# The last state's transposes behind the next batch's late neighbours: an order change in a graph-attention and GRU kernel

## The chip, the cores and the metric

The kernel runs on one core of a Trainium2 chip. The metric is the device time of one launch in microseconds (us). The engines have a queue each and run beside one another: TensorE (PE, with its weight loads as PEld), VectorE (DVE), ScalarE (ACT), GpSimd (POOL), and SyncE (SP), which here issues all DMAs. An instruction that waits for a semaphore holds up everything behind it on its engine.

## The reference

Eight batches of a graph with 1024 nodes and 128 features each. `x` is a layer-norm and ReLU away from a graph attention; its result is added to `x`; the sum goes through a layer-norm and ReLU into three gated graph layers with a GRU cell; and the last state is added again.

```python
h = jnp.maximum(_layernorm(x), 0.0)
Wh = h @ W
e = leaky(e_i[:, :, None] + e_j[:, None, :])       # e_i = Wh.a1, e_j = Wh.a2, slope 0.2
attention = softmax(where(adj > 0, e, -9e15), axis=2)
x = x + elu(attention @ Wh)
h = jnp.maximum(_layernorm(x), 0.0)                # h0 below
A = (adj != 0)
for i in range(3):
    aggr = einsum('bst,bsd->btd', A, h @ weight[i])
    r, z = sigmoid(i_r + h_r), sigmoid(i_z + h_z)  # gi = aggr @ w_ih.T + b_ih, gh = h @ w_hh.T + b_hh
    n = tanh(i_n + r * h_n)
    h = (1 - z) * n + z * h
x = x + h
```

## The kernel before, in words

Work is written by hand, one program for each engine, each with a `first()` for what comes ahead and a `body(b, ...)` that is run for the eight batches. The order of the calls in `body` is the order on the engine; semaphores with counts join the engines. Body `b` does the three GRU layers of batch `b` and, between them, the attention of the next batch `a = b + 1` and the first steps of batch `b + 2`. `attend` is true while there is a batch `a` (all but the last body), `prepare` while there is a batch `b + 2` (bodies 0 to 5).

A batch is 8 tiles of 128 nodes, or two halves of 512 (`c` = 0 and 1). In the GRU the state is kept with features on partitions (`hkT`, and `h0T` for the first), split into a high and a low part for exact matmuls. One layer goes: the neighbours' sum `ps_g` (16 matmuls of 128x512 for each half of source tiles: `neighbours(b, par, l, k, c)` takes source half `k` to target half `c`, 8 matmuls), its split (`g_hi` on ACT, `g_lo_half` on DVE), nine matmuls of the old state and nine of the sum for each half (`gates_h`, `gates_g`), the gates (`r_gate`, `z_gate`, `n_gate` on ACT, `n_input` on DVE), `z_times_h` on POOL, `new_h` on DVE, which writes `hkT`, and the transpose back (`h_back` on PE). After the last layer the transposed halves go into PSUM banks `ps_hn` and `ps_r`, and `out_half` on DVE adds `x1` and leaves the output for the store. The next batch's first nine state matmuls write `ps_hn` again and wait until both `out_half` are done.

The end of a body, called the tail here, is where the GRU of batch `b` ends and that of `a` begins. For the second half of `a`'s first state it runs: `att_half`, `x1_sum` (DVE, the residual), `norm2` (DVE, statistics), `rstd2_half` (POOL, with a power), `h0_half` (ACT), then `split_h0` (DVE) for the neighbour matmuls and `h0T_half` (PE transposes, ACT copy) with `split_h` (POOL) for the state matmuls. In `neighbours(a, a_par, 0, k, c)` the source half `k = 0` ("early") needs the first half of `h0`, and `k = 1` ("late") the second.

Around the tail stand attention steps of batch `b + 2`: `leaky_tile` (ACT) writes a tile of scores, `away_tile` (DVE) makes the mask from the adjacency, `scores` (DVE) adds them and takes the row maximum, `exp_tile` (ACT) follows, and `probT_tile` transposes on PE. `norm1` (DVE) and `rstd1` (POOL) are the first layer-norm of batch `b + 2`. Lines of the profile that matter: L969 neighbours, L912 transposes, L978 to L980 gate matmuls; L646 away, L652 edges, L662 scores, L698 and L704 statistics of `norm2`, L714 and L716 `split_h0`, L721 `g_lo`, L727 and L730 `n_input`, L737 and L740 `new_h`, L751 `out_half`; L366 `h0_half`; L275 to L280 `rstd_of`, L300 and L302 `z_times_h`, L312 and L315 `split_h`.

Of the kernel before, what the change touches and what calls it, by code (L numbers as in the profile page):

```python
# [21 lines left out]
def gat_gru_kernel(nc, x, adj, gat_w, gat_a, layer_w, w_ih, w_hh, b_ih, b_hh, out):  # L22
# [6 lines left out]
    QS = 2 * L  # L29
# [9 lines left out]
    with ExitStack() as ctx:  # L39
# [224 lines left out]
        @block.gpsimd  # L264
        def _(pool):
            pool.memset(minus_half[:], -0.5)
            pool.memset(ident[:], 0.0).then_inc(const_done, 1)
            pool.wait_ge(const_done, 1)
            pool.affine_select(out=ident[:], in_=ident[:], compare_op=ALU.not_equal, fill=1.0, base=0,
                               pattern=[[-1, P]], channel_multiplier=1).then_inc(const_done, 1)  # L270
            pool.wait_ge(const_done, 2)

            def rstd_of(dst, minus, mean_var, k, n, added, powered, done):

                pool.tensor_scalar(dst, mean_var[:, :, 1], LN_EPS, 1.0, ALU.add, ALU.mult).then_inc(added, 1)  # L275
                pool.tensor_scalar(minus, mean_var[:, :, 0], -1.0, 0.0, ALU.mult, ALU.add)
                pool.wait_ge(added, n)
                pool.tensor_tensor(dst, dst, minus_half[:, 0:k], ALU.pow).then_inc(powered, 1)  # L278
                pool.wait_ge(powered, n)
                pool.tensor_tensor(minus, minus, dst, ALU.mult).then_inc(done, 1)  # L280

            def rstd1(b):
                pool.wait_ge(mv_done, b + 1)
                if b > 0:
                    pool.wait_ge(h_done, b * 2)
                rstd_of(rstd[:], shift[:], mv, T, b + 1, vare_done, pow_done, rstd_done)

            def rstd2_half(b, c):
                n = b * 2 + c + 1
                pool.wait_ge(mv2_done, n)  # L290
                if n > 1:
                    pool.wait_ge(h0_done, n - 1)
                rstd_of(rstd2[:], shift2[:], mv2, TH, n, vare2_done, pow2_done, rstd2_done)

            def z_times_h(b, l, c):

                n = b * QS + 2 * l + c + 1
                h = h0T if l == 0 else hkT
                pool.wait_ge(tz_done, n)
                pool.tensor_scalar(tz[c][:], tz[c][:], 0.5, 0.5, ALU.mult, ALU.add).then_inc(z_done, 1)  # L300
                pool.wait_ge(z_done, n)
                pool.tensor_tensor(zh[c][:], tz[c][:], h[:, cols(c)], ALU.mult).then_inc(zh_done, 1)  # L302

            def split_h(b, l, c):

                n = b * QS + 2 * l + c + 1
                h = h0T if l == 0 else hkT
                if l == 0:
                    pool.wait_ge(h0T_done, b * 2 + c + 1)
                else:  # L310
                    pool.wait_ge(hk_done, n - 2)
                pool.tensor_scalar(hT_hi[:, cols(c)], h[:, cols(c)], 1.0, 0.0, ALU.mult, ALU.add  # L312
                                   ).then_inc(hT_hi_done, 1)
                pool.wait_ge(hT_hi_done, n)
                pool.tensor_tensor(hT_lo[:, cols(c)], h[:, cols(c)], hT_hi[:, cols(c)], ALU.subtract  # L315
                                   ).then_inc(hT_lo_done, 1)

            def first():
                rstd1(0)
                rstd1(1)  # L320
                rstd2_half(0, 0)
                split_h(0, 0, 0)
                rstd2_half(0, 1)
                split_h(0, 0, 1)

            def body(b, par, attend, prepare):
                if prepare:
                    rstd1(b + 2)
                for l in range(L - 1):
                    z_times_h(b, l, 0)  # L330
                    z_times_h(b, l, 1)
                    split_h(b, l + 1, 0)
                    split_h(b, l + 1, 1)
                if attend:
                    rstd2_half(b + 1, 0)
                z_times_h(b, L - 1, 0)
                z_times_h(b, L - 1, 1)
                if attend:
                    rstd2_half(b + 1, 1)
                    split_h(b + 1, 0, 0)  # L340
                    split_h(b + 1, 0, 1)

            run(pool, first, body)


        @block.scalar
        def _(act):
# [10 lines left out]
            def h0_half(b, par, c):  # L358

                n = b * 2 + c + 1  # L360
                act.wait_ge(rstd2_done, n)
                if n > 1:
                    act.wait_ge(h0T_ps, n - 1)
                    act.wait_ge(h0_lo_done, n - 1)
                for t in range(TH):
                    last = act.activation(h0[:, t, :], x1[par][:, c * TH + t, :], ACT.Relu, bias=shift2[:, t:t + 1],  # L366
                                          scale=rstd2[:, t:t + 1])
                last.then_inc(h0_done, 1)
# [55 lines left out]
            def r_gate(b, l, c):  # L424

                act.wait_ge(r_ps, b * QS + 2 * l + c + 1)
                act.activation(tr[c][:], ps_r[:], ACT.Tanh, bias=b_rz[:, 0:1], scale=0.5).then_inc(tr_done, 1)  # L427

            def z_gate(b, l, c):
                act.wait_ge(z_ps, b * QS + 2 * l + c + 1)  # L430
                act.activation(tz[c][:], ps_z[:], ACT.Tanh, bias=b_rz[:, 1:2], scale=0.5).then_inc(tz_done, 1)  # L431

            def n_gate(b, l, c):
                if l == 0:
                    act.wait_ge(stored[c], b * 16 + 1)
                act.wait_ge(pre_done, b * QS + 2 * l + c + 1)
                act.activation(nn[c][:], pre[c][:], ACT.Tanh, bias=bih_in[:, 2:3]).then_inc(n_done, 1)  # L437
# [36 lines left out]
            def body(b, par, attend, prepare):  # L474
# [88 lines left out]
                r_gate(b, 2, 0)  # L563
                z_gate(b, 2, 0)
                hnb_half(b, 2, 1)
                n_gate(b, 2, 0)
                r_gate(b, 2, 1)
                z_gate(b, 2, 1)
                n_gate(b, 2, 1)
                if prepare:  # L570
                    leaky_tile(b + 2, par, 0)
                if attend:
                    h0_half(a, a_par, 1)
                    h0T_half(a, a_par, 1)
                if prepare:
                    leaky_tile(b + 2, par, 1)
# [5 lines left out]
        def _(dve):  # L582
# [66 lines left out]
            def edge_tile(b, par, t):  # L649


                dve.tensor_scalar(edges[par][:, t, :], adj_in[t % TA][:], 0.0, None, ALU.not_equal  # L652
                                  ).then_inc(edges_done, 1)
# [76 lines left out]
                dve.tensor_tensor(pre[c][:], pre[c][:], ps_in[:], ALU.add).then_inc(pre_done, 1)  # L730

            def new_h(b, l, c):

                n = b * QS + 2 * l + c + 1
                dve.wait_ge(z_done, n)
                dve.wait_ge(n_done, n)
                dve.scalar_tensor_tensor(nn[c][:], tz[c][:], 1.0, nn[c][:], ALU.subtract, ALU.mult).then_inc(zn_done, 1)  # L737
                dve.wait_ge(zn_done, n)
                dve.wait_ge(zh_done, n)
                dve.tensor_tensor(hkT[:, cols(c)], zh[c][:], nn[c][:], ALU.subtract).then_inc(hk_done, 1)  # L740
# [38 lines left out]
            def body(b, par, attend, prepare):  # L779
                a, a_par = b + 1, 1 - par  # L780

                if attend:
                    scores(a, 0)
                    away_tile(a, a_par, 1)
                    scores(a, 1)
                if prepare:
                    norm1(b + 2, par)
# [56 lines left out]
                g_lo_half(b, 2, 1)  # L844
                if attend:
                    split_h0(a, 0)
                    att_half(a, a_par, 1)
                    x1_sum(a, a_par, 1)
                n_input(b, 2, 0)
                if attend:  # L850
                    norm2(a, a_par, 1)
                    new_h(b, 2, 0)
                    n_input(b, 2, 1)
                else:
                    new_h(b, 2, 0)
                    n_input(b, 2, 1)
                new_h(b, 2, 1)
                if attend:
                    split_h0(a, 1)
                out_half(b, par, 0)  # L860
                if prepare:
                    away_tile(b + 2, par, 0)
                out_half(b, par, 1)

            run(dve, first, body)

# [2 lines left out]
        def _(pe):  # L869
# [191 lines left out]
            def body(b, par, attend, prepare):  # L1061
# [10 lines left out]
                    neighbours(b, par, l, 1, 1)  # L1072


                late_neighbours(0)
                if attend:
                    probT_tile(a, a_par, 0)
                gates_h(b, 0, 0)
# [51 lines left out]
                gates_g(b, 2, 0)  # L1130
                gates_h(b, 2, 1)
                gates_g(b, 2, 1)
                h_back(b, 2, 0)
                if attend:
                    neighbours(a, a_par, 0, 0, 0)
                h_back(b, 2, 1)
                if attend:
                    neighbours(a, a_par, 0, 0, 1)
                    h0T_half(a, a_par, 1)

            run(pe, first, body)


# [23 lines left out]
```

## Time and profile before

| | |
|---|---|
| median of 3 runs | 695.64 us (695.63 to 695.66) |
| the profiled execution's own time | 695.68 us |
| its span, first to last instruction | 693.9 us |
| PE busy | 623.9 us (90%) |
| DVE busy | 521.4 us (75%) |
| ACT busy | 453.2 us (65%) |
| POOL busy | 282.2 us (41%) |

Times inside the trace are from the start of the span. Matmuls are pipelined: one of 128x512 is shown with about 0.40 us, and the next starts some 0.24 us after it. In a row of the order of time the second column is the duration, and the bracket at the end is how long the engine stood idle before the row, and what ended that.

### The profile page before, as it was taken

The page shows a single profiled execution, that of the slowest core. Times are in us where ns is not written, and L with a number is a line of the kernel's source. Part 1 is how long each engine was busy: PE and PEld are TensorE (multiplying, and loading weights), DVE is VectorE, ACT ScalarE, POOL GpSimd, SP SyncE. Part 2 cuts the span into 40 slices and gives each one's busy share as a digit, 9 for nine tenths or more (in the row PEclk, how much of TensorE's full clock was granted, in tenths as well). Part 3 has the DMA queues.
Part 4 walks back from the last instruction along what each step waited for, and adds up shares of the span by engine and source line. Part 5 has one row for each costly group of instructions (what it writes and reads, how often), then busy time and mean ns, then how long its engine had stood idle before and what let it go on. Part 6 is the DMA issues. An engine that isn't in the chain of part 4 may idle for free.

```text
span 693.9 us, 8823 instructions
## 1 busy us (share of the span) xinstructions
PE 623.9 (90%) x2845; PEld 457.0 (66%) x2845; DVE 521.4 (75%) x1218; ACT 453.2 (65%) x777; POOL 282.2 (41%) x295
## 2 busy tenths in 40 slices
PE   2687899989999899988999889997999899998996
PEld 2465677667686676666776666866766677766774
DVE  5766998489876898669985798768986689656544
ACT  2784786558874678557864588756785577554443
POOL 1203544166242561544442662425615434425442
PEclk9999999999999999999999999999999999999999
DMA  6521130122302132022401223021320131001001
GB/s 222 180 92 61 44 139 31 47 77 92 112 10 92 31 122 92 31 62 67 146 32 45 78 92 95 28 91 31 121 92 27 34 94 60 0 1 30 1 1 30
DMA packets 28670, 47.40 MB, mean 68 GB/s; under 512 B 1672, under 2 KB 19408, under 8 KB 28624
## 3 DMA queue, kind: packets, MB, share of 16 engines
q1 hardware_dynamic: 28624, 46.84, 20.3%
q8 instruction: 23, 0.38, 0.2%
q14 instruction: 23, 0.19, 0.1%
HBM read 42.60 MB, written 4.23 MB: 67 GB/s over the span
## 4 chain that ended last, share of the span: by engine, by line
PE 52%; DVE 20%; ACT 11%; POOL 10%; issue 5%; DMA 1%; DVEq 0%; POOLq 0%; ACTq 0%
PE ps_x L931 14%; PE ps_g L969 8%; PE ps_x L912 6%; DVE score L662 4%; POOL rstd L278 3%; DVE away L646 3%; POOL zh L302 3%; DVE hkT L740 2%; ACT score L390 2%; PE ps_r L978 2%; PE ps_r L980 2%; PE ps_r L979 2%; DVE nn L737 2%; PE ps_z L978 2%; PE ps_z L979 2%
## 5 line engine op out<-in xcount | busy, mean ns | idle before, releaser
L969 PE MATMUL ps_g<-edges,h_hi 128*128 128x512 f32 x384 | 157.8, 411 | 11.7 <-DVE h_lo L746 6.6
L969 PE MATMUL ps_g<-edges,h_lo 128*128 128x512 f32 x384 | 151.9, 396 | 0.0
L300 POOL TENSOR_SCALAR tz<-tz 128x512 f32<-128x512 f32 x48 | 37.0, 771 | 253.8 <-ACT tz L431 253.8
L390 ACT ACTIVATE score<-score,nmax 128x1024 f32<-128x1024 f32 x64 | 73.8, 1153 | 43.8 <-DVE nmax L662 42.8
L931 PE MATMUL ps_x<-probT,h_nat 128*128 128x512 f32 x224 | 98.9, 594 | 0.0
L662 DVE CUSTOM_DVE_ANT_0 score<-score,away 128x1024 f32<-128x1024 f32 x64 | 89.0, 1390 | 8.0 <-ACT score L384 7.0
L969 PEld LDWEIGHTS ps_g<-edges,h_hi 128*128 128x128 f32 x384 | 72.8, 189 | 31.2 <-DVE h_lo L746 10.3
L912 PE MATMUL ps_x<-ident,score 128*128 128x128 f32 x512 | 71.6, 282 | 17.4 <-ACT score L390 16.2
L397 ACT ACTIVATE probT<-ps_x 128x512 f32<-128x512 f32 x128 | 71.0, 597 | 17.3 <-PE ps_x L912 17.2
L969 PEld LDWEIGHTS ps_g<-edges,h_lo 128*128 128x128 f32 x384 | 72.9, 190 | 13.6
L912 PEld LDWEIGHTS ps_x<-ident,score 128*128 128x128 f32 x512 | 59.4, 145 | 34.1 <-ACT score L390 25.4
L384 ACT ACTIVATE score<-ej,ei 128x1024 f32<-128x1024 f32 x64 | 73.0, 1143 | 6.0 <-DMA ej<-ej_kept_at 5.0
L931 PEld LDWEIGHTS ps_x<-probT,h_nat 128*128 128x128 f32 x224 | 41.9, 190 | 50.3 <-issue 46.9
L646 DVE TENSOR_SCALAR away<-adj_in 128x1024 bf16<-128x1024 int32 x64 | 61.6, 963 | 0.0
L315 POOL TENSOR_TENSOR hT_lo<-hkT,hT_hi 128x512 fp32r<-128x512 f32 x32 | 56.9, 1777 | 2.7
L275 POOL TENSOR_SCALAR rstd<-mv 128x4 f32<-128x4 f32 (+1 forms) x24 | 7.5, 312 | 122.5 <-DVE mv L704 75.1
L737 DVE SCALAR_TENSOR_TENSOR nn<-tz,nn 128x512 f32<-128x512 f32 x48 | 37.2, 775 | 24.0 <-ACT nn L437 24.0
L437 ACT ACTIVATE nn<-tr,vec 128x512 f32<-128x512 f32 x48 | 34.8, 725 | 28.0 <-DVE tr L730 26.7
L652 DVE TENSOR_SCALAR edges<-adj_in 128x1024 fp32r<-128x1024 int32 x64 | 50.6, 799 | 0.0
L366 ACT ACTIVATE h<-x,shift,rstd 128x128 f32<-128x128 f32 x64 | 26.4, 482 | 32.5 <-POOL shift L280 32.5
L721 DVE TENSOR_TENSOR g_lo<-ps_g,g_hi 128x512 fp32r<-128x512 f32 x48 | 31.6, 680 | 19.7 <-ACT g_hi L417 19.7
L727 DVE SCALAR_TENSOR_TENSOR tr<-tr,hnb 128x512 f32<-128x512 f32 x48 | 35.9, 748 | 11.7 <-ACT tr L427 11.6
(133 smaller groups left out, 1314.0 us busy)
## 6 DMA issues: line engine op xcount, KB each, us to landing
adj_in<-in_adj SPq DMA_DIRECT2D x64, 512.0 KB, 3.3
x_nat<-in_x SPq DMA_DIRECT2D x8, 512.0 KB, 4.7
ej<-ej_kept_at SPq DMA_DIRECT2D x8, 512.0 KB, 3.6
out<-nn SPq DMA_DIRECT2D x16, 256.0 KB, 2.3
probT<-in_L_gnn_weight SPq DMA_DIRECT2D x1, 192.0 KB
probT<-in_L_gnn_w_ih SPq DMA_DIRECT2D x1, 192.0 KB
probT<-in_L_gnn_w_hh SPq DMA_DIRECT2D x1, 192.0 KB
ej_kept_at<-ej_row SPq DMA_DIRECT2D x8, 4.0 KB
```

Source lines behind the costliest of these rows:

```text
L300: pool.tensor_scalar(tz[c][:], tz[c][:], 0.5, 0.5, ALU.mult, ALU.add).then_inc(z_done, 1)
L315: pool.tensor_tensor(hT_lo[:, cols(c)], h[:, cols(c)], hT_hi[:, cols(c)], ALU.subtract).then_inc(hT_lo_done, 1)
L384: act.activation(score[t % U][:], ej[:], ACT.Prelu, bias=ei[par][:, t:t + 1], alpha=SLOPE).then_inc(leaky_done, 1)
L390: act.activation(score[t % U][:], score[t % U][:], ACT.Exp, bias=nmax[:, t:t + 1], scale=-1.0, accum_out=rowsum[:, t:t + 1]).then_inc(exp_ ...
L397: act.activation(probT[:, k * TH:(k + 1) * TH, tile_cols(t % TH)], bank_of("probT", 2 * t + k, par)[:].rearrange("p (j i) -> p j i", j=TH) ...
L646: dve.tensor_scalar(away[t % 2][:], adj_in[t % TA][:], 0.0, -K, ALU.is_le, ALU.mult).then_inc(away_done, 1)
L652: dve.tensor_scalar(edges[par][:, t, :], adj_in[t % TA][:], 0.0, None, ALU.not_equal).then_inc(edges_done, 1)
L662: dve.tensor_tensor_reduce(u[:], u[:], away[t % 2][:], -1.0, FLT_BIG, ALU.add, ALU.min, nmax[:, t:t + 1]).then_inc(max_done, 1)
L737: dve.scalar_tensor_tensor(nn[c][:], tz[c][:], 1.0, nn[c][:], ALU.subtract, ALU.mult).then_inc(zn_done, 1)
L912: last = pe.transpose(dst[:, tile_cols(t)], src, ident[:])
L931: last = pe.matmul(bank_of("agg", c, par)[:], h_nat[par][:, j, :], probT[:, j, :], start=(j == 0), stop=(j == T - 1))
L969: last = pe.matmul(ps_g[c][:], part[:, s, :], edges[par][:, s, cols(c)], start=(s == 0 and part is h_hi), stop=(s == T - 1 and part is h_lo))
```

## The change

Nothing is computed that was not computed before; calls move. On PE the two `h_back` of the last layer leave the tail of body `b` and stand in body `b + 1`, each behind one half of the late neighbours. On POOL the second `rstd2_half` goes ahead of both `z_times_h`. On ACT `h0_half(a, a_par, 1)` goes ahead of the second `n_gate`, and the first `n_gate` behind the second `r_gate`. On DVE the second `norm2` follows its `x1_sum` at once, `new_h` of the last layer's first half is cut in two with `split_h0(a, 1)` between, `scores(b + 2, 0)` comes ahead of the last `new_h`, `away_tile(b + 2, 0)` goes ahead of the second `att_half`, and both `out_half` go to the next body, the second behind `away_tile(a, a_par, 1)`. In layer 0 one `edge_tile` goes behind `new_h`.

```diff
 # POOL
                 if attend:
                     rstd2_half(b + 1, 0)
+                if attend:
+                    rstd2_half(b + 1, 1)
                 z_times_h(b, L - 1, 0)
                 z_times_h(b, L - 1, 1)
                 if attend:
-                    rstd2_half(b + 1, 1)
                     split_h(b + 1, 0, 0)
 # ACT (condition on attend left out of n_gate)
-                n_gate(b, 2, 0)
                 r_gate(b, 2, 1)
+                    n_gate(b, 2, 0)
                 z_gate(b, 2, 1)
+                if attend:
+                    h0_half(a, a_par, 1)
                 n_gate(b, 2, 1)
                 if prepare:
                     leaky_tile(b + 2, par, 0)
                 if attend:
-                    h0_half(a, a_par, 1)
                     h0T_half(a, a_par, 1)
 # DVE, start of the body
-                if attend:
+                if b == 0:
                     scores(a, 0)
+                else:
+                    out_half(b - 1, a_par, 0)
+                if attend:
                     away_tile(a, a_par, 1)
+                if b > 0:
+                    out_half(b - 1, a_par, 1)
+                if attend:
                     scores(a, 1)
...
                     edge_tile(a, a_par, 1)
+                new_h(b, 0, 0)
+                if attend:
                     edge_tile(a, a_par, 2)
-                new_h(b, 0, 0)
 # DVE, tail
+                if prepare:
+                    away_tile(b + 2, par, 0)
+                if attend:
                     att_half(a, a_par, 1)
-                    x1_sum(a, a_par, 1)
-                n_input(b, 2, 0)
-                if attend:
-                    norm2(a, a_par, 1)
+                    x1_half(a, a_par, 1)
+                    n_input(b, 2, 0)
+                    n_input(b, 2, 1)
+                    n_part(b, 2, 0)
+                    split_h0(a, 1)
+                    h_sum(b, 2, 0)
...
+                if prepare:
+                    scores(b + 2, 0)
                 new_h(b, 2, 1)
-                if attend:
-                    split_h0(a, 1)
-                out_half(b, par, 0)
-                if prepare:
-                    away_tile(b + 2, par, 0)
-                out_half(b, par, 1)
+                if not attend:
+                    out_half(b, par, 0)
+                    out_half(b, par, 1)
 # PE, start of the body
-                late_neighbours(0)
+                neighbours(b, par, 0, 1, 0)
+                if b > 0:
+                    h_back(b - 1, 2, 0)
+                neighbours(b, par, 0, 1, 1)
+                if b > 0:
+                    h_back(b - 1, 2, 1)
 # PE, tail
-                h_back(b, 2, 0)
                 if attend:
                     neighbours(a, a_par, 0, 0, 0)
-                h_back(b, 2, 1)
-                if attend:
                     neighbours(a, a_par, 0, 0, 1)
                     h0T_half(a, a_par, 1)
```

PE in the tail of body 0, from the last gate matmul to the first score transposes of the next body, before (`ps_hn` and `ps_r` take the old batch's transposes, `ps_x1` those of `h0`; of each run of eight neighbour matmuls the first stands):

```order
L980 MATMUL ps_in<-g_hi1,cT_lo 128x512
L912 MATMUL ps_hn<-ident,hkT 128x128 x4
L969 MATMUL ps_g0<-edges1,h_hi 128x512
...
L912 MATMUL ps_r<-ident,hkT 128x128 x4
L969 MATMUL ps_g1<-edges1,h_hi 128x512
...
L912 MATMUL ps_x1<-ident,h0 128x128 x4
...
L912 MATMUL ps_x0<-ident,score0 128x128 x4
```

The same place of the changed program, where the lines are numbered 23 higher:

```order
L1003 MATMUL ps_in<-g_hi1,cT_lo 128x512
L992 MATMUL ps_g0<-edges1,h_hi 128x512
...
L935 MATMUL ps_x1<-ident,h0 128x128 x4
L992 MATMUL ps_g0<-edges1,h_hi 128x512
...
L935 MATMUL ps_hn<-ident,hkT 128x128 x4
L992 MATMUL ps_g1<-edges1,h_hi 128x512
...
L935 MATMUL ps_r<-ident,hkT 128x128 x4
L935 MATMUL ps_x0<-ident,score0 128x128 x4
```

All 16 early neighbour matmuls now come directly behind the gates, and the two groups of `hkT` transposes behind eight late ones each.

DVE at the same place before, from the first half's `new_h` (`nn0`, `hkT<-zh0`) to the next batch's first `scores`:

```order
L737 SCALAR_TENSOR_TENSOR nn0<-tz0,nn0 128x512
L740 TENSOR_TENSOR hkT<-zh0,nn0 128x512
L727 SCALAR_TENSOR_TENSOR tr1<-tr1,hnb1 128x512
L730 TENSOR_TENSOR tr1<-tr1,ps_in 128x512
L737 SCALAR_TENSOR_TENSOR nn1<-tz1,nn1 128x512
L740 TENSOR_TENSOR hkT<-zh1,nn1 128x512
L714 TENSOR_SCALAR h_hi<-h0 128x512
L716 TENSOR_TENSOR h_lo<-h0,h_hi 128x512
L751 TENSOR_TENSOR nn0<-ps_hn,x1_0 128x512
L646 TENSOR_SCALAR away0<-adj_in0 128x1024
L751 TENSOR_TENSOR nn1<-ps_r,x1_0 128x512
L662 ISA score0,nmax<-score0,away0 128x1024
```

And in the changed program, from the second half's `n_input` to the second output sum:

```order
L735 TENSOR_TENSOR tr1<-tr1,ps_in 128x512
L746 SCALAR_TENSOR_TENSOR nn0<-tz0,nn0 128x512
L719 TENSOR_SCALAR h_hi<-h0 128x512
L721 TENSOR_TENSOR h_lo<-h0,h_hi 128x512
L753 TENSOR_TENSOR hkT<-zh0,nn0 128x512
L667 ISA score0,nmax<-score0,away0 128x1024
L667 ISA nmax 128x1
L746 SCALAR_TENSOR_TENSOR nn1<-tz1,nn1 128x512
L753 TENSOR_TENSOR hkT<-zh1,nn1 128x512
L764 TENSOR_TENSOR nn0<-ps_hn,x1_0 128x512
L651 TENSOR_SCALAR away1<-adj_in1 128x1024
L764 TENSOR_TENSOR nn1<-ps_r,x1_0 128x512
```

The split of `h0` comes ahead of both `hkT` halves, the first score ahead of the second half's `new_h`, and the mask between the output sums is that of tile 1 instead of tile 0.

## Rows read from the trace of the kernel before

**Rows 1.** Stretches: length, then PE, PEld, DVE, ACT, POOL busy us (count), clock, DMA.

```profile
231.20:240.20 9.00, 7.49 (x38) 5.79 (x38) 8.86 (x26) 5.59 (x9) 2.50 (x3) 1.00 0.22 60
240.20:264.10 23.90, 22.38 (x111) 17.35 (x110) 23.44 (x34) 20.19 (x36) 13.61 (x12) 1.00 0.34 113
264.10:300.00 35.90, 35.86 (x158) 24.10 (x157) 23.81 (x74) 22.08 (x41) 11.69 (x12) 1.00 0.12 45
```

**Rows 2.** PE by time, tail of the second body: start, us, engine, line, [idle before].

```profile
225.14 0.66 PE L912 MATMUL ps_hn<-ident,hkT 128*128 128x128 f32 x4 [0.38 <-DVE hkT L740]
225.55 0.48 PE L969 MATMUL ps_g<-edges,h_hi 128*128 128x512 f32 x1
...
229.16 0.66 PE L912 MATMUL ps_r<-ident,hkT 128*128 128x128 f32 x4 [1.50 <-DVE hkT L740]
...
232.55 0.50 PE L969 MATMUL ps_g<-edges,h_hi 128*128 128x512 f32 x1 [0.46 <-DVE h_lo L716]
...
237.54 1.09 PE L912 MATMUL ps_x<-ident,score 128*128 128x128 f32 x8 [1.05 <-ACT score L390]
...
240.95 0.50 PE L978 MATMUL ps_r<-g_hi,cT_hi 128*128 128x512 f32 x1 [0.22 <-DVE g_lo L721]
```

**Rows 3.** DVE by time, the same tail.

```profile
218.02 1.13 DVE L674 TENSOR_SCALAR att<-ps_x,rinv 128x128 f32<-128x128 f32 x4 [2.85 <-PE ps_x L952]
...
221.18 0.68 DVE L727 SCALAR_TENSOR_TENSOR tr<-tr,hnb 128x512 f32<-128x512 f32 x1
...
222.50 0.86 DVE L698 BATCH_NORM_STATS2 stats<-x 128x6 f32<-128x128 f32 x4
223.40 0.38 DVE L704 BATCH_NORM_AGGREGATE mv<-stats 128x2 f32<-128x6 f32 x4
...
227.68 0.69 DVE L737 SCALAR_TENSOR_TENSOR nn<-tz,nn 128x512 f32<-128x512 f32 x1 [0.86 <-ACT nn L437]
...
231.24 0.53 DVE L714 TENSOR_SCALAR h_hi<-h 128x512 fp32r<-128x512 f32 x1 [2.14 <-ACT h L366]
...
232.41 0.68 DVE L751 TENSOR_TENSOR nn<-ps_hn,x 128x512 f32<-128x512 f32 x1
233.01 0.96 DVE L646 TENSOR_SCALAR away<-adj_in 128x1024 bf16<-128x1024 int32 x1
...
234.49 1.72 DVE L662 CUSTOM_DVE_ANT_0 score<-score,away 128x1024 f32<-128x1024 f32 x1
...
236.85 1.23 DVE L662 CUSTOM_DVE_ANT_0 score<-score,away 128x1024 f32<-128x1024 f32 x1
238.00 0.08 DVE L662 DVE_READ_ACCUMULATOR2_ANT nmax<- 128x1 f32 x1
...
240.24 1.25 DVE L721 TENSOR_TENSOR g_lo<-ps_g,g_hi 128x512 fp32r<-128x512 f32 x2
```

**Rows 4.** ACT by time, the same tail.

```profile
224.10 0.69 ACT L431 ACTIVATE tz<-ps_z,b_rz 128x512 f32<-128x512 f32 x1
...
227.48 1.13 ACT L384 ACTIVATE score<-ej,ei 128x1024 f32<-128x1024 f32 x1
229.55 1.65 ACT L366 ACTIVATE h<-x,shift,rstd 128x128 f32<-128x128 f32 x4 [0.94 <-POOL shift L280]
```

**Rows 5.** POOL by time, the same tail.

```profile
222.43 1.30 POOL L302 TENSOR_TENSOR zh<-tz,hkT 128x512 f32<-128x512 f32 x1
...
227.34 0.19 POOL L275 TENSOR_SCALAR rstd<-mv 128x4 f32<-128x4 f32 x1
```

**Rows 6.** DVE by time, layer 0 of the third body: a mask.

```profile
252.84 1.77 DVE L646 TENSOR_SCALAR away<-adj_in 128x1024 bf16<-128x1024 int32 x1
```

**Rows 7.** POOL by time, the same moment.

```profile
252.46 1.59 POOL L315 TENSOR_TENSOR hT_lo<-hkT,hT_hi 128x512 fp32r<-128x512 f32 x1
```

**Rows 8.** PE by time, the last tail.

```profile
629.09 0.39 PE L980 MATMUL ps_in<-g_hi,cT_lo 128*128 128x512 f32 x1
...
641.07 0.39 PE L978 MATMUL ps_hn<-hT_hi,whhT_hi 128*128 128x512 f32 x1
```

More of the change, by code:

```diff
@@ L565, in body @@
                 hnb_half(b, 2, 1)
-                n_gate(b, 2, 0)
+                if not attend:
+                    n_gate(b, 2, 0)
                 r_gate(b, 2, 1)
+                if attend:
+                    n_gate(b, 2, 0)
                 z_gate(b, 2, 1)
+                if attend:
+                    h0_half(a, a_par, 1)
                 n_gate(b, 2, 1)
@@ L732, in new_h, with n_part @@
             def new_h(b, l, c):
+                n_part(b, l, c)
+                h_sum(b, l, c)
+            def n_part(b, l, c):
                 n = b * QS + 2 * l + c + 1
@@ L737, in new_h, with h_sum @@
                 dve.scalar_tensor_tensor(nn[c][:], tz[c][:], 1.0, nn[c][:], ALU.subtract, ALU.mult).then_inc(zn_done, 1)
+            def h_sum(b, l, c):
+                n = b * QS + 2 * l + c + 1
                 dve.wait_ge(zn_done, n)
@@ L780, in body @@
                 a, a_par = b + 1, 1 - par
+                if b == 0:
+                    scores(a, 0)
+                else:
+                    out_half(b - 1, a_par, 0)
                 if attend:
-                    scores(a, 0)
                     away_tile(a, a_par, 1)
+                if b > 0:
+                    out_half(b - 1, a_par, 1)
+                if attend:
                     scores(a, 1)
@@ L846, in body @@
                     split_h0(a, 0)
+                if prepare:
+                    away_tile(b + 2, par, 0)
+                if attend:
                     att_half(a, a_par, 1)
-                    x1_sum(a, a_par, 1)
-                n_input(b, 2, 0)
-                if attend:
-                    norm2(a, a_par, 1)
+                    x1_half(a, a_par, 1)
[4 more added lines that the diff above has]
+                    h_sum(b, 2, 0)
+                else:
+                    n_input(b, 2, 0)
                     new_h(b, 2, 0)
                     n_input(b, 2, 1)
-                else:
-                    new_h(b, 2, 0)
-                    n_input(b, 2, 1)
+                if prepare:
+                    scores(b + 2, 0)
                 new_h(b, 2, 1)
-                if attend:
-                    split_h0(a, 1)
-                out_half(b, par, 0)
-                if prepare:
-                    away_tile(b + 2, par, 0)
-                out_half(b, par, 1)
+                if not attend:
+                    out_half(b, par, 0)
+                    out_half(b, par, 1)
             run(dve, first, body)
@@ L1132, in body @@
                 gates_g(b, 2, 1)
-                h_back(b, 2, 0)
                 if attend:
                     neighbours(a, a_par, 0, 0, 0)
-                h_back(b, 2, 1)
-                if attend:
                     neighbours(a, a_par, 0, 0, 1)
                     h0T_half(a, a_par, 1)
+                else:
+                    h_back(b, 2, 0)
+                    h_back(b, 2, 1)
             run(pe, first, body)
```

## The prediction

> **What bounds the kernel now.** I read the busy time by stretches first. From 264 to 300 us of the third body PE has no idle time (35.86 of 35.90 us). From 240 to 264 it stands 1.5 us, and there DVE is full (23.44 of 23.90); from 231 to 240 DVE is full too (8.86 of 9.00), while PE idles 1.5 us [rows 1]. So a body is bound by PE for its later part, and by DVE for some 33 us from the end of the tail on. The granted clock is at its upper level in each stretch.
>
> Next I read PE in order of time through the tail of the second body, which stands for all seven tails (bodies 0 to 6). PE waits five times: 0.38 and 1.50 us for `hkT`, 0.46 for the split `h0`, 1.05 for the first exponential, 0.22 for `g_lo` [rows 2]; together 3.6 us. The last wait is short, but it ends last: whatever PE gains earlier, the first gate matmul on `g` (240.95) cannot start before DVE's first `g_lo` (240.24) is done.
>
> So DVE's own row of work decides. It waits 2.14 us for the second half of `h0` until 231.24, and from there it works without a pause to `g_lo` [rows 3]: 9.0 us for the split, two output sums, a mask, two scores, a mask and the statistics of `norm1`. The half of `h0` is late because ACT writes it at 229.55 to 231.20 [rows 4], behind POOL's `rstd2`, which starts only at 227.34 [rows 5], though its statistics are ready at 223.78 (223.40 and 0.38, [rows 3]): POOL does both `z_times_h` first.
>
> **The change, part by part.** Times are those of this tail, so a difference is a gain per tail.
>
> *The second half of h0.* `norm2` no longer stands behind `n_input`, which took from 221.18 to 222.50 [rows 3], so the statistics end 1.3 us earlier, at 222.5. POOL takes them at once; its four instructions and the hand-over to ACT take 2.2 us (227.34 to 229.55, [rows 4, 5]): 224.7. ACT is not free then. Its second `z_gate`, 224.10 to 224.79 [rows 4], now has a tanh of the same size ahead of it and ends near 225.5; with 1.65 us, `h0` is done near 227.2 instead of 231.2, 4 us earlier. Queued behind it on ACT are the second `n_gate` and the first leaky tile (1.13 us, [rows 4]), which end about 229.0. On POOL both `z_times_h` move behind `rstd2`: about 0.7 and 1.3 us each [rows 5], so near 227 and 229.
>
> *PE.* Sixteen matmuls from 232.55 end at 236.49 (237.54 less 1.05), so one starts 0.236 us after another ((3.94 - 0.40) / 15), and four transposes take 0.41 (225.14 to 225.55) [rows 2]. The gates can be followed at 224.60 (225.14 less 0.38, less 0.16 by which the last matmul's modelled 0.40 overlaps the next). Now come 16 early matmuls (3.78) to 228.4, the `h0` transposes to 228.8, eight late ones to 230.7, the first `hkT` transposes to 231.1, eight late ones to 233.0, and the second `hkT` transposes, which end 0.66 later, 233.6. Nothing in this row has to wait: `h0` is there at 227.2, its split (1.17 us on DVE, 231.24 to 232.41) at 228.4, 0.4 before the late ones. The waits of 0.38, 1.50 and 0.46 go; the new places of the `hkT` transposes cost no instruction.
>
> *DVE.* Behind `h0` at 227.2 now stand: the split (1.17), the first half's difference (0.69 like its neighbour at 227.68), the first score (1.15 as at 236.85 to 238.00, or the 1.72 of the row at 234.49), the second half's `new_h` (two of 0.69), the first output sum (0.60), a mask (0.96) [rows 3]. That ends between 233.1 and 233.7, just when PE's last transposes do (233.6). From there the order leaves no choice: output sum 0.68, score 1.15, `norm1` 2.24 (238.00 to 240.24), and `g_lo` starts at 237.8 instead of 240.24: 2.4 to 2.5 us earlier. PE would come to it at about 236.5 (probabilities 0.85, nine state matmuls 2.1), so I expect a new wait of about 2 us there in place of the 0.22. The state matmuls also wait for the second output sum, by some 0.2 us.
>
> *The mask of tile 0* (0.96) goes ahead of `att_half`, where DVE stands idle 2.85 us for PE [rows 3]: nothing, and nothing if the cover shrank by half. Without cover it costs 0.96 per tail.
>
> *The edge tile behind new_h of layer 0* is in DVE's full stretch: the same instructions in another order, so zero for `g`. Bounds: PE could get `hkT` one edge tile (0.7) earlier, or the next `n_input` be 0.7 later; I take zero, since DVE has no gap to give.
>
> *DMAs.* None is added. The two output stores are issued in the next body, ahead of the next adjacency load as before, and that load waits for edges that DVE makes only after `g_lo`. I take nothing.
>
> *Collisions of DVE and POOL.* A mask at 252.84 takes 1.77 us instead of 0.96 or less, beside a POOL subtraction at 252.46 to 254.05 [rows 6, 7], so a full collision costs DVE 0.8 to 1.1 us; the score at 234.49 is 0.5 over the one at 236.85. In the new order POOL works from 224.7 to about 233 without a gap (two `z_times_h`, two `split_h`, each about 2 us), and DVE's split, difference, score, `new_h` and mask lie beside it. Before, the same stretch had idle time of DVE beside `split_h`. Some of it is in the sum already (1.72, 0.96); the bounds of the rest are -0.9 (the collisions of the layer behind lapse, by re-phasing) and +1.9 (two more full ones). I take 0.3, near to the partial ones that this tail shows.
>
> By the Trainium skill (SBUF — State Buffer, "Who interferes with whom") whichever of a VectorE instruction with two SBUF inputs, or in a two-port mode, and a GpSimd instruction comes first holds their shared ports, and the other blocks until it is done. The 1.77 us agree with that. By the rule alone all four 1.3 us POOL products and subtractions could each hold up one DVE instruction; with two more of 1.3 than now nothing of a tail's 2.5 would be left but the last tail's 2.0, about 693.7 by this estimate.
>
> *Sum.* 2.5 - 0.3 = 2.2 us in each of the six tails with a batch `b + 2`: 13.2. The last tail has no score, mask or `norm1`. There PE is behind the gates at 629.32 (629.09 + 0.39 - 0.16); the same row of matmuls brings its second `hkT` transposes to 637.7, their end to 638.4, the output sum to 639.1, and the state matmuls start there instead of at 641.07 [rows 8]: 2.0. The first body's start and the last batch keep their order. Together 15.2 us of the profiled execution's 695.68 (span 693.9, and 1.8 around it, which stay): 680.5. The median of the runs is 0.04 below that execution, which changes nothing.
>
> **The rivals.**
>
> *More gain.* If no collision is left in the new tail and the shifted phase also loosens those in layer 0, a tail gives up to 3.3 us: 6 x 3.3 + 2.0 = 21.8, 673.9 us. For it: 1 us and more stands in single stretched rows. Against: PE's transposes at 233.6 and the 4.1 us of DVE work behind them are a floor for `g_lo`, so 2.5 is all that the tail itself can give.
>
> *Collisions take it.* One to two more full ones in DVE's row (0.9 each) leave about 1.2 a tail: 6 x 1.2 + 2.0 = 9.2, 686.5 us. For it: POOL now runs right through that row. Against: the first score has 0.4 us of slack before PE's transposes are done, and the second score and `norm1` come when POOL is through.
>
> *It doesn't matter.* The body is paced elsewhere (the adjacency loads, the row of `ej`), and what the tail gives is waited for later: 695. Against: no DMA ends a wait of PE or DVE in these stretches.
>
> *Slower.* In the new order 10.3 us of DVE work stand between `h0` and `g_lo` (1.17 + 0.69 + 1.4 + 1.4 + 0.6 + 0.96 + 0.68 + 1.15 + 2.24), before 9.0. It decides against the change from the point where `h0` is less than 1.3 us earlier than now, after 229.9. If `h0` stayed at 231.2, because ACT held it up behind the gates or POOL's power came late again, each of the six tails would lose 1.3 us: 695.7 + 7.8 = 703.5 with nothing gained in the last. Against: three engines would each have to add a microsecond.
>
> **How the numbers follow.** My forecast, 1.8 to 2.6 us a tail (its own range 678.1 to 682.9): 62%. More gain: 12%. Collisions take most: 18%. No difference: 3%. Slower: 5%. A measurement of this kernel can tell 0.2% (1.4 us) from no change. Faster is thus 92%, the same 3%, slower 5%. The range takes most of the second and third case: 675 to 687.
>
> **What would show it.** PE: the waits of 1.50 and 0.46 gone, `hkT` transposes without a wait or with a few tenths; a wait of 1.5 to 2.3 us for `g_lo` in the first gate matmul, six times. DVE: the wait for `h0` under 1 us. ACT: `h0_half` ending near 227.2 on this tail's clock, and hardly a wait for `rstd2`. POOL: no wait for DVE's statistics longer than 1 us. The prediction is wrong if `h0` is later than 230, if the second `hkT` half comes after PE wants it (233.0) by more than 0.7, or if the gain is seen in the tail and waited for again after 240.

## The result, and the profile of the changed kernel

The changed kernel takes 697.82 us (median of 7 runs), the kernel before 695.66: ratio 1.0029, interval 1.002 to 1.0039. It is slower by 0.2 to 0.4%, where 680.5 (675 to 687) had been forecast. The profiled span went from 693.9 to 696.0 us. The granted clock does not explain it: a run of the changed kernel at 0.994 took 698.58, one at 0.986 took 697.82, and in the 20 us behind the last gate matmul it is 1.00 in all seven tails of both kernels.

Page of the changed kernel, busy time by engine and two groups of DVE (line, instruction | busy, mean ns):

```profile
PE 624.0 (90%) x2845; PEld 457.6 (66%) x2845; DVE 547.5 (79%) x1218; ACT 452.3 (65%) x777; POOL 293.2 (42%) x295
...
L746 DVE SCALAR_TENSOR_TENSOR nn<-tz,nn 128x512 f32<-128x512 f32 x48 | 48.5, 1011 | 19.0 <-ACT nn L438 19.0
...
L753 DVE TENSOR_TENSOR hkT<-zh,nn 128x512 f32<-128x512 f32 x48 | 46.7, 973 | 1.4
```

DVE runs the same 1218 instructions but is busy 547.5 us instead of 521.4. `nn<-tz,nn` means 1011 ns instead of 775, `hkT<-zh,nn` 973 instead of 789. Instructions have become longer, and the tail shows which. Line numbers are higher than before by 23 on PE, 5 to 13 on DVE and 1 on ACT; times below are again of the second body's tail, where the last gate matmul starts at 224.75 (before 224.37, 0.38 earlier).

PE by time, the rows of the tail with a wait (they answer to [rows 2]):

```profile
230.12 0.50 PE L992 MATMUL ps_g<-edges,h_hi 128*128 128x512 f32 x1 [0.86 <-DVE h_lo L721]
...
236.08 0.66 PE L935 MATMUL ps_r<-ident,hkT 128*128 128x128 f32 x4 [1.55 <-DVE hkT L753]
...
237.88 0.50 PE L1001 MATMUL ps_hn<-hT_hi,whhT_hi 128*128 128x512 f32 x1 [0.27 <-DVE nn L764]
...
241.83 0.50 PE L1001 MATMUL ps_r<-g_hi,cT_hi 128*128 128x512 f32 x1 [1.59 <-DVE g_lo L726]
```

All four are for DVE, 4.3 us together where there were 3.6. The `hkT` transposes wait 1.55 us in a place where they were to come without a wait, and the first gate matmul on `g` starts 17.08 us behind the last gate matmul, before 16.58 (240.95 less 224.37).

DVE by time, from the last `n_input` sum to `g_lo` (answers to [rows 3]):

```profile
225.25 0.69 DVE L735 TENSOR_TENSOR tr<-tr,ps_in 128x512 f32<-128x512 f32 x1 [0.21 <-PE ps_in L1003]
225.85 1.76 DVE L746 SCALAR_TENSOR_TENSOR nn<-tz,nn 128x512 f32<-128x512 f32 x1
227.54 0.85 DVE L719 TENSOR_SCALAR h_hi<-h 128x512 fp32r<-128x512 f32 x1
228.42 1.64 DVE L721 TENSOR_TENSOR h_lo<-h,h_hi 128x512 fp32r<-128x512 f32 x1
229.99 1.09 DVE L753 TENSOR_TENSOR hkT<-zh,nn 128x512 f32<-128x512 f32 x1
231.00 2.32 DVE L667 CUSTOM_DVE_ANT_0 score<-score,away 128x1024 f32<-128x1024 f32 x1
...
233.25 1.09 DVE L746 SCALAR_TENSOR_TENSOR nn<-tz,nn 128x512 f32<-128x512 f32 x1
234.38 1.65 DVE L753 TENSOR_TENSOR hkT<-zh,nn 128x512 f32<-128x512 f32 x1
235.94 0.68 DVE L764 TENSOR_TENSOR nn<-ps_hn,x 128x512 f32<-128x512 f32 x1
...
237.14 0.68 DVE L764 TENSOR_TENSOR nn<-ps_r,x 128x512 f32<-128x512 f32 x1
...
241.11 1.26 DVE L726 TENSOR_TENSOR g_lo<-ps_g,g_hi 128x512 fp32r<-128x512 f32 x2
```

And POOL beside it (answers to [rows 5]):

```profile
222.91 0.54 POOL L275 TENSOR_SCALAR rstd<-mv 128x4 f32<-128x4 f32 x1 [10.46 <-DVE mv L709]
...
225.06 0.62 POOL L300 TENSOR_SCALAR tz<-tz 128x512 f32<-128x512 f32 x1
225.77 1.30 POOL L302 TENSOR_TENSOR zh<-tz,hkT 128x512 f32<-128x512 f32 x1
227.03 1.07 POOL L300 TENSOR_SCALAR tz<-tz 128x512 f32<-128x512 f32 x1
228.19 1.33 POOL L302 TENSOR_TENSOR zh<-tz,hkT 128x512 f32<-128x512 f32 x1
229.49 1.06 POOL L312 TENSOR_SCALAR hT_hi<-h0T 128x512 fp32r<-128x512 f32 x1
230.63 1.62 POOL L315 TENSOR_TENSOR hT_lo<-h0T,hT_hi 128x512 fp32r<-128x512 f32 x1
232.21 1.59 POOL L312 TENSOR_SCALAR hT_hi<-h0T 128x512 fp32r<-128x512 f32 x1
233.89 1.59 POOL L315 TENSOR_TENSOR hT_lo<-h0T,hT_hi 128x512 fp32r<-128x512 f32 x1
```

Read the two in pairs. From 225.77 on POOL works without a gap until 235.48, and its seven large instructions lie beside seven of DVE's, one to one. Beside the four with two inputs (1.30 to 1.62) DVE's `nn`, `h_lo`, score and `hkT` take 1.76, 1.64, 2.32, 1.65, where rows without POOL give 0.69 and, for the score, 1.22: 1.07 + 0.95 + 1.10 + 0.96 = 4.1 us. Beside the three with one input (1.07, 1.06, 1.59) DVE's `h_hi`, `hkT`, `nn` take 0.85, 1.09, 1.09 instead of 0.43 and 0.69: 1.2 us. Together 5.3 us in one tail. As POOL ends, DVE's instructions are short again.

The ends of the fourteen instructions (start plus duration) alternate strictly: POOL 227.07, DVE 227.61, POOL 228.10, DVE 228.39, and so on to POOL 235.48 and DVE 236.03. Each end comes a little less behind the other engine's than the instruction takes alone (DVE 0.53 to 0.55 us, `h_hi` 0.29, the score 1.07; POOL 0.48 or 0.49 with one input, 1.13 to 1.17 with two). So the 10.3 us from 225.77 to 236.03 are the sum of what the two do one after the other, about 6.2 of POOL and 4.1 of DVE.

The whole program agrees. The score transposes ahead of layer 1's state matmuls of one body and the next were 81.16 us apart before and are 81.83 apart now, in five bodies: +3.4. The start gives 0.44 back, the sixth period 0.52, the end 0.34: +2.1, the 696.0 less 693.9 of the spans. Of the 0.67 a body, 0.50 are there at the first gate matmul on `g`.

### The profile page after: what moved, and what is told of

It reads as the page before. It is cut to its first block, busy times and chain, and to the rows that moved or that the text cites. A ratio compares the mean times of both kernels' runs of the same rounds, so it can differ in the third digit from the quotient of the medians.

```text
span 696.0 us, 8823 instructions
## 1 busy us (share of the span) xinstructions
PE 624.0 (90%) x2845; PEld 457.6 (66%) x2845; DVE 547.5 (79%) x1218; ACT 452.3 (65%) x777; POOL 293.2 (42%) x295
## 3 DMA queue, kind: packets, MB, share of 16 engines
HBM read 42.60 MB, written 4.23 MB: 67 GB/s over the span
## 4 chain that ended last, share of the span: by engine, by line
PE 46%; DVE 28%; POOL 11%; ACT 9%; issue 5%; DMA 1%; DVEq 0%; ACTq 0%; POOLq 0%
PE ps_x L954 14%; PE ps_g L992 9%; DVE score L667 5%; PE ps_x L935 5%; DVE hkT L753 5%; POOL zh L302 4%; DVE nn L746 3%; POOL rstd L278 3%; ACT score L391 2%; POOL tz L300 2%; PE ps_x L975 2%; DVE away L651 2%; DVE stats L626 2%; PE ps_r L1001 2%; PE ps_z L1001 2%
## 5 line engine op out<-in xcount | busy, mean ns | idle before, releaser
L300 POOL TENSOR_SCALAR tz<-tz 128x512 f32<-128x512 f32 x48 | 38.8, 807 | 179.6 <-ACT tz L432 179.6
L667 DVE CUSTOM_DVE_ANT_0 score<-score,away 128x1024 f32<-128x1024 f32 x64 | 93.2, 1456 | 7.1 <-ACT score L385 6.3
L275 POOL TENSOR_SCALAR rstd<-mv 128x4 f32<-128x4 f32 (+1 forms) x24 | 9.9, 414 | 196.6 <-DVE mv L709 147.7
L746 DVE SCALAR_TENSOR_TENSOR nn<-tz,nn 128x512 f32<-128x512 f32 x48 | 48.5, 1011 | 19.0 <-ACT nn L438 19.0
L651 DVE TENSOR_SCALAR away<-adj_in 128x1024 bf16<-128x1024 int32 x64 | 59.2, 925 | 0.0
L753 DVE TENSOR_TENSOR hkT<-zh,nn 128x512 f32<-128x512 f32 x48 | 46.7, 973 | 1.4
L428 ACT ACTIVATE tr<-ps_r,b_rz 128x512 f32<-128x512 f32 x48 | 33.0, 688 | 21.9 <-PE ps_r L1003 21.9
L732 DVE SCALAR_TENSOR_TENSOR tr<-tr,hnb 128x512 f32<-128x512 f32 x48 | 32.9, 686 | 13.8 <-ACT tr L428 13.8
```

What stands on the lines that cost most here:

```text
L651: dve.tensor_scalar(away[t % 2][:], adj_in[t % TA][:], 0.0, -K, ALU.is_le, ALU.mult).then_inc(away_done, 1)
L667: dve.tensor_tensor_reduce(u[:], u[:], away[t % 2][:], -1.0, FLT_BIG, ALU.add, ALU.min, nmax[:, t:t + 1]).then_inc(max_done, 1)
```

## Experiments

Theory C (collisions): the tail would give what was forecast, but DVE and POOL hold each other up. Rivals: the edge tile moved in layer 0 costs it (E), or the new order itself is too long for DVE and no collision matters (the prediction's own "slower"). All ratios are to the kernel before, run alongside (medians 695.82 to 696.12 us).

**1 to 3: POOL's work made short.** The diff is against the changed kernel; the three differ in which of the four calls get the width 16. They leave out most of `z*h`, of the split, or of both, and serve to measure, not to be used.

```diff
-                z_times_h(b, L - 1, 0)
-                z_times_h(b, L - 1, 1)
+                z_times_h(b, L - 1, 0, 16 if attend else HALF)   # 1, 2
+                z_times_h(b, L - 1, 1, 16 if attend else HALF)   # 1, 2
                 if attend:
-                    split_h(b + 1, 0, 0)
-                    split_h(b + 1, 0, 1)
+                    split_h(b + 1, 0, 0, 16)   # 1, 3
+                    split_h(b + 1, 0, 1, 16)   # 1, 3
```

Both short (1): 

> The changed kernel, with the POOL instructions of the tail (the last layer's two z_times_h of bodies 0 to 6, and the two split_h of the next batch's first state) cut from 512 to 16 columns; this leaves out most of z*h and of the state's split there. Collision theory: DVE's ten instructions from the first half's product to the last new_h lose their 5.3 us of stretching a tail, g_lo starts when PE's last transposes allow it (2.5 us earlier than in the kernel before), 677 to 681 us. Rival, the order itself: the DVE row behind h0 is longer by 1.3 us and PE waits for it whatever POOL does, 694 to 698 us.

Products alone (2): 

> As x1_pool_short, but only the two z_times_h of the tail are cut to 16 columns (leaves out most of z*h there); the splits are whole. Collision theory: the two collisions of the products (the first half's product in DVE 1.76 us instead of 0.68, the split of h0 2.4 instead of 1.2) go, those of the two splits (score and last new_h) stay in part: 682 to 688 us. If the products alone were the loss: 677 to 679. If they were nothing: 696 to 698.

Splits alone (3): 

> As x1_pool_short, but only the two split_h are cut to 16 columns (leaves out most of the split of the state there). Collision theory: DVE is where it was up to the split of h0, then its first score loses 1.1 us and its last new_h 1.3, so g_lo starts about 2.4 us earlier: 680 to 685 us. If the splits alone were the loss: 677 to 679. If they were nothing: 696 to 698.

Measured: 677.42 us, ratio 0.9738 (0.9724 to 0.9753); 683.09, 0.9814 (0.9798 to 0.983); 684.85, 0.9842 (0.9828 to 0.9857). DVE by time with both short:

```profile
223.01 0.68 DVE L748 SCALAR_TENSOR_TENSOR nn<-tz,nn 128x512 f32<-128x512 f32 x1
224.25 0.43 DVE L721 TENSOR_SCALAR h_hi<-h 128x512 fp32r<-128x512 f32 x1 [0.55 <-ACT h L369]
224.71 0.69 DVE L723 TENSOR_TENSOR h_lo<-h,h_hi 128x512 fp32r<-128x512 f32 x1
225.32 0.68 DVE L755 TENSOR_TENSOR hkT<-zh,nn 128x512 f32<-128x512 f32 x1
226.01 1.22 DVE L669 CUSTOM_DVE_ANT_0 score<-score,away 128x1024 f32<-128x1024 f32 x1
...
227.16 0.70 DVE L748 SCALAR_TENSOR_TENSOR nn<-tz,nn 128x512 f32<-128x512 f32 x1
227.90 0.69 DVE L755 TENSOR_TENSOR hkT<-zh,nn 128x512 f32<-128x512 f32 x1
...
231.03 0.69 DVE L766 TENSOR_TENSOR nn<-ps_r,x 128x512 f32<-128x512 f32 x1 [1.00 <-PE ps_r L937]
...
235.01 1.26 DVE L728 TENSOR_TENSOR g_lo<-ps_g,g_hi 128x512 fp32r<-128x512 f32 x2
```

Every one of the seven instructions is short, and DVE now waits for PE (1.00), so PE's row of matmuls is the floor there, as the prediction had it. `g_lo` starts 13.1 us behind the last gate matmul (221.90), before 15.87: 2.76 us gained in a tail. This shows theory C, and refutes E and the too long order: both are still in this kernel. In 2 the splits still stretch `h_lo`, `nn` and `hkT` (1.67, 1.09, 1.67), in 3 the products stretch `nn`, `h_hi` and `h_lo` (1.78, 0.84, 1.65). The splits that are left in 2 cost 5.7 us of the program (683.09 less 677.42), the products left in 3 cost 7.4, both together 20.4: the two alone don't add up to both, and the likely reason, not tested by itself, is that the first part of any stretching falls into DVE's waits for ACT and PE (0.55 and 1.00 above).

**4: the edge tile put back.**

```diff
-                new_h(b, 0, 0)
                 if attend:
                     edge_tile(a, a_par, 2)
+                new_h(b, 0, 0)
```

> The changed kernel with layer 0's third edge tile ahead of new_h again. Collision theory: DVE is full there, the order inside makes nothing, 697 to 698.5 us. Rival, that this move is the loss (PE's wait for the first h_lo of layer 0 grew from 0.54 to 1.00 us): 694 to 695 us.

Measured 697.83, ratio 1.0029 (1.0018 to 1.004): as the changed kernel. The move costs and gives nothing that these runs can tell.

**5 and 6: `rstd2` behind the first product, and behind both as before.**

```diff
                     rstd2_half(b + 1, 0)
+                z_times_h(b, L - 1, 0)
                 if attend:
                     rstd2_half(b + 1, 1)
-                z_times_h(b, L - 1, 0)
                 z_times_h(b, L - 1, 1)
```

The diff is that of 5; 6 puts the second `rstd2_half` behind both products.

Behind the first (5): 

> The changed kernel with POOL's second rstd2_half between the two z_times_h instead of ahead of both. Collision theory: the first product lies beside DVE's reads of PSUM and costs nothing there, POOL is through with its row some 2 us earlier, h0 comes only 0.5 us later; two collisions of 1 us fewer, so 6 x 1.3 to 2 us less: 686 to 690 us. Rival, the order itself: h0 0.5 to 1 us later is all that changes, 700 to 703 us.

Behind both (6): 

> The changed kernel with POOL's order of the kernel before (rstd2_half behind both z_times_h). Collision theory: h0 comes near 231.3 again, but now 10.3 us of DVE work stand behind it; POOL's splits still lie beside them: 700 to 706 us. Rival, that POOL's new order is the whole loss: 688 to 694 us.

Measured 696.45, ratio 1.0006 (0.9997 to 1.0016), and 719.36, 1.034 (1.0324 to 1.0356). Both numbers lie outside the ranges of either side. POOL's product and DVE with one product ahead:

```profile
222.54 1.29 POOL L302 TENSOR_TENSOR zh<-tz,hkT 128x512 f32<-128x512 f32 x1
...
222.80 1.58 DVE L732 SCALAR_TENSOR_TENSOR tr<-tr,hnb 128x512 f32<-128x512 f32 x1
...
230.07 1.78 DVE L753 TENSOR_TENSOR hkT<-zh,nn 128x512 f32<-128x512 f32 x1
231.78 1.63 DVE L667 CUSTOM_DVE_ANT_0 score<-score,away 128x1024 f32<-128x1024 f32 x1
...
233.34 1.78 DVE L746 SCALAR_TENSOR_TENSOR nn<-tz,nn 128x512 f32<-128x512 f32 x1
```

The product has only moved to another victim: at 222.54 to 223.83 it stretches `n_input` (0.66 to 1.58), whose sum PE's `n` gates wait for (0.80), so all behind them is 0.9 later; six more instructions are still stretched (0.84 to 1.78 us, the three longest above). With both ahead the same happens, and DVE then stands 4.67 us for `h0`:

```profile
235.51 0.49 DVE L718 TENSOR_SCALAR h_hi<-h 128x512 fp32r<-128x512 f32 x1 [4.67 <-ACT h L366]
```

since ACT, which now has `h0_half` ahead of the second `n_gate`, waits 4.23 us for `rstd2`. So POOL's part of the change is needed by ACT's part. Part of the 719.36 is PE's clock. PE in 6:

```profile
235.62 1.08 PE L934 MATMUL ps_x<-ident,h 128*128 128x128 f32 x4 [2.66 <-ACT h L366]
...
237.38 0.63 PE L991 MATMUL ps_g<-edges,h_lo 128*128 128x512 f32 x1
237.80 0.63 PE L991 MATMUL ps_g<-edges,h_hi 128*128 128x512 f32 x1
```

Behind the 2.66 us without work the granted clock is 0.50 up to 240 (1.2 GHz in place of 2.4), and the late matmuls start 0.43 us apart instead of 0.23. From the first late matmul to the second `hkT` transposes PE takes 6.56 us (236.78 to 243.34), in experiment 11 4.24 (226.56 to 230.80), and DVE waits 0.25 and 1.23 us for the two groups of transposes. Over the 20 us behind the gates the clock is 0.83 to 0.91 in six of the seven tails.

**7 and 8: parts of the change alone, on the kernel before.** 7 moves only the mask of tile 0 ahead of `att_half`; 8 has only PE's moved `hkT` transposes, with the output sums that need them:

```diff
 # 7, DVE
                     split_h0(a, 0)
+                if prepare:
+                    away_tile(b + 2, par, 0)
...
                 out_half(b, par, 0)
-                if prepare:
-                    away_tile(b + 2, par, 0)
                 out_half(b, par, 1)
 # 8, PE
-                late_neighbours(0)
+                neighbours(b, par, 0, 1, 0)
+                if b > 0:
+                    h_back(b - 1, 2, 0)
...
```

7: 

> The kernel before with one part of the change: the mask of tile 0 of batch b + 2 goes ahead of the second att_half, into DVE's wait for PE. DVE's full stretch behind h0 is 0.9 us shorter in six tails: 690 to 691.5 us. If PE's waits for hkT and h0 decided and not DVE's row: 695 to 696.

8: 

> The kernel before with the part of the change that its few words put first: h_back behind the late neighbours on PE, both out_half in the next body on DVE (behind them the first score and the next mask); POOL, ACT and the rest of DVE as before. PE's waits of 0.38 and 1.50 us for hkT go, but DVE's row behind h0 is as long and now also waits for PE's later transposes: 697 to 706 us. If PE's waits were worth what they last: 683 to 686.

Measured 694.43, ratio 0.9976 (0.9967 to 0.9985), and 714.61, 1.0266 (1.0252 to 1.028): 7 gained a third of what was expected, 8 lost more. DVE in 7:

```profile
233.66 2.28 DVE L662 CUSTOM_DVE_ANT_0 score<-score,away 128x1024 f32<-128x1024 f32 x1
```

Without the mask the score starts beside POOL's last subtraction (233.56, 1.30 us) and takes 2.28 instead of 1.72: `g_lo` starts 15.56 us behind the last gate matmul (239.98 less 224.42), before 15.87: 0.31 gained, not 0.96. DVE in 8:

```profile
239.65 0.69 DVE L751 TENSOR_TENSOR nn<-ps_hn,x 128x512 f32<-128x512 f32 x1 [3.08 <-PE ps_hn L918]
```

Here `h0` is as late as before, and the transposes stand behind neighbours that need it, so the output sums, the score behind them and ACT's first exponential (3.93 us for it) all wait. About 1.0 of the 3.08 us is again PE's clock: PE stands 2.85 us for `h0`, the clock is 0.50 from 235 to 238, and the first late half takes 2.99 us up to the `hkT` transposes (236.03 to 239.02), in experiment 11 1.94 (226.56 to 228.50). With `h0` this late, PE's part by itself costs 2.7%.

**9 to 11: the whole computation, with POOL's work elsewhere.** 9 puts the first `split_h` ahead of `rstd2` on POOL, where POOL waits for the statistics. 10 takes layer 0's `split_h` from POOL: ACT copies `hT_hi`, DVE subtracts. 11 does that and gives DVE the tail's two products:

```diff
 # 9, POOL
+                    split_h(b + 1, 0, 0)
                     rstd2_half(b + 1, 1)
...
-                    split_h(b + 1, 0, 0)
                     split_h(b + 1, 0, 1)
 # 10 and 11, POOL
-                    split_h(b + 1, 0, 0)
-                    split_h(b + 1, 0, 1)
 # 11, DVE, in n_part (10 and 11 also have DVE's hT_lo<-h0T,hT_hi)
                 dve.scalar_tensor_tensor(nn[c][:], tz[c][:], 1.0, ...
+                if l == L - 1 and b + 1 < B:
+                    dve.tensor_tensor(zh[c][:], tz[c][:], hkT[:, cols(c)], ALU.mult).then_inc(zh_done, 1)
```

9: 

> The changed kernel with POOL's split of the state's first half ahead of the second rstd2_half, where POOL waits for the statistics and DVE does statistics and reads of PSUM. Collision theory: two of POOL's eight large instructions leave the stretch, DVE's score or last new_h loses 1.3 to 1.7 us: 686 to 690 us. Rival, that early POOL work only delays rstd2 and h0: 697 to 700 us.

10: 

> The changed kernel with the tail's split of the state taken from POOL: ACT writes hT_hi straight from PSUM ahead of its copy of h0T, DVE the difference hT_lo (the first half between the two n_input, the second between the mask of tile 1 and the second output sum). All is computed. Collision theory: two DVE instructions of 0.6 us more, but the collisions of the splits go: g_lo about 2.1 us earlier, 682 to 687 us. Rival, that DVE's amount of work decides: 1.2 us more a tail, 702 to 706 us.

11: 

> As x7_split_act_dve, and the tail's two products z*h also go from POOL to DVE (each behind the product of n), so POOL has only rstd2 and the two small affine steps there; ACT makes the first half of hT_hi behind its last hnb instead of ahead of the r gate. All is computed. Collision theory: the 2.5 us that the products still cost DVE in x7 go for two instructions of 0.6 us, most of it where DVE waits for h0 or for PE: 677 to 682 us. Rival, that DVE's amount of work decides: no less than x7's 687.5.

Measured: 690.68, ratio 0.9926 (0.9911 to 0.9941); 687.53, 0.9881 (0.9867 to 0.9896); 679.26, 0.9759 (0.9745 to 0.9772). 9 and 10 lie 0.5 to 0.7 above their ranges. In 9 the early split stretches the sum ahead of the statistics (0.98) and five instructions of the tail stay long (`nn` 1.64 and 1.77, `h_hi` 0.84, `h_lo` 1.65, score 1.63); in 10 the products still stretch `nn`, `h_hi` and `h_lo` (1.76, 0.85, 1.65). 11 beats both kernels. DVE in 11, from the first difference to the second output sum:

```profile
223.56 1.10 DVE L759 SCALAR_TENSOR_TENSOR nn<-tz,nn 128x512 f32<-128x512 f32 x1
224.58 0.68 DVE L761 TENSOR_TENSOR zh<-tz,hkT 128x512 f32<-128x512 f32 x1
225.18 0.41 DVE L726 TENSOR_SCALAR h_hi<-h 128x512 fp32r<-128x512 f32 x1
225.63 0.69 DVE L728 TENSOR_TENSOR h_lo<-h,h_hi 128x512 fp32r<-128x512 f32 x1
226.24 0.69 DVE L768 TENSOR_TENSOR hkT<-zh,nn 128x512 f32<-128x512 f32 x1
226.84 1.22 DVE L674 CUSTOM_DVE_ANT_0 score<-score,away 128x1024 f32<-128x1024 f32 x1
...
231.79 0.69 DVE L779 TENSOR_TENSOR nn<-ps_r,x 128x512 f32<-128x512 f32 x1
...
235.77 1.25 DVE L739 TENSOR_TENSOR g_lo<-ps_g,g_hi 128x512 fp32r<-128x512 f32 x2
```

DVE has four instructions more in a tail, 0.6 us each from start to start (one 0.8), and is done earlier than in the changed kernel: only one instruction is still long (1.10, beside POOL's `tz`). `g_lo` starts 13.47 us behind the last gate matmul (222.30): 2.4 a tail, the gain that the prediction worked out before collisions. A product that costs DVE 0.6 cost it 0.95 to 1.07 when POOL did it alongside.

## Why the prediction was wrong

The step that failed is the term "Collisions of DVE and POOL", taken as 0.3 us a tail and bounded at 1.9. Measured are 5.3 us of stretching in the tail, where the tail before has about 1.3 (`tr` 0.40, `h_hi` 0.10, the mask 0.27, the score 0.50 over short rows). What this is worth shows at `g_lo`: forecast 13.4 us behind the last gate matmul (237.8 less 224.37) ahead of this term, it starts at 13.11 in experiment 1 and at 16.36 in the changed kernel (241.11 less 224.75): 3.25 a tail. The prediction saw that POOL would work without a gap from 224.7 to about 233 beside DVE's row, and had the price of a full collision (0.8 to 1.1, [rows 6, 7]); it then took the size from the tail of before, where most of that POOL work lay beside DVE's idle time, its statistics or its reads of PSUM. Counting would have given most of it: four POOL instructions with two inputs at about 1.0 us. The price of the three with one input, about 0.4, was in none of its rows.

- **The second half of `h0`**: right. Forecast near 227.2, 227.6 on this run's gates, and ACT:

```profile
225.40 1.64 ACT L367 ACTIVATE h<-x,shift,rstd 128x128 f32<-128x128 f32 x4
```

  done at 227.04, without a wait for `rstd2`. But the split starts only at 227.54, as the difference ahead of it is itself stretched.
- **PE's row**: right as a floor. In experiment 1

```profile
230.39 0.60 PE L937 MATMUL ps_r<-ident,hkT 128*128 128x128 f32 x4
```

  the second `hkT` transposes start 8.5 us behind the start of the last gate matmul (230.39 less 221.90), forecast 8.6 (233.0 less 224.37). In the changed kernel DVE didn't serve it (0.86 and 1.55 of waits).
- **DVE's row**: the second output sum was to start at 233.6, 234.0 on this run's gates; it starts at 237.14, 3.2 later. From there to `g_lo` it takes 3.97 us, forecast 4.1. The new wait for `g_lo`, about 2, is 1.59.
- **The mask at nothing, the edge tile at zero, no DMA effect**: experiment 4 bears out the edge tile. Where the mask went, DVE still has idle time behind it (0.70 us at 220.09), but experiment 7 shows that leaving its place moves the score into a collision. No wait of PE in the tail ends on a DMA.
- **The last tail, 2.0 us**: 1.0. The state matmuls start 11.02 us behind the last gate matmul (642.72 less 631.70), before 11.98 [rows 8]; the same collisions stand there.
- **The sum**: with collisions gone the rest holds. Experiment 1 gives 677.4 and experiment 11 679.3, forecast 680.5 (678.7 without the 0.3).
- **The rivals**: "Collisions take it" had the mechanism, with one or two full ones instead of seven partial and full ones, so 686.5 was too low. "Slower" (`h0` no earlier) had the sign by another mechanism, and `h0` was early. By the rule of the Trainium skill (SBUF — State Buffer, "Who interferes with whom") the estimate was 693.7, nearer than 686.5; the trace agrees with the rule in the seven pairs of a tail, where DVE's instruction ends only behind POOL's. The estimate was low because it took two holds more than before, none of them by POOL's instructions with one input, and 2.0 us from the last tail, which gave 1.0.

## What to carry to other kernels

Before filling an engine's idle time, lay the new order of DVE and POOL side by side and count the pairs that both work on SBUF: in this kernel each large pair cost DVE 0.4 or about 1.0 us, and a stretch that was full on both took the sum of their work. POOL's work was cheap beside DVE's waits and, by one overlap, beside its reads of PSUM; beside a DVE row that decides, a product that DVE does in 0.6 us was better done by DVE itself (experiment 11, 679.3 us, against 10, 687.5). And a move that frees a place shifts everything behind it into other neighbours, so the price is to be read from the new pairs, not from the old rows.

## What the runs showed of the hardware

- POOL's instructions with one input hold DVE up too: `h_hi` 0.43 to 0.85, `nn` and `hkT` 0.69 to 1.09, and they themselves grow from 0.62 to 1.06 or 1.59.
- The custom score instruction is stretched as well, 1.22 to 2.32 or 2.28.
- POOL waits for DVE too: in experiment 1 its 128x16 product takes 0.72 us at 223.06, beside DVE's `nn` (223.01 to 223.69), and 0.22 at 222.53.
- A DVE sum that reads PSUM was not stretched beside POOL: `tr<-tr,ps_in` at 225.25 took 0.69 while POOL's `tz` ran from 225.06, and that `tz` kept its 0.62. One overlap shows this, no more.
- POOL's small power instruction (128x4, 1.01 us at 223.69) left the DVE instruction beside it at 0.69 (224.35), and in the kernel before one of 1.47 us at 227.76 left two at 0.69 (227.68 and 228.41).
- PE's granted clock fell to 0.50 behind 2.66 and 2.85 us without work (experiments 6 and 8, this tail).
